# The threshold search of a two-step graph kernel: its second choice, its interpolation and its narrowing made by GpSimd on single columns

## What is computed

```
h = relu(layernorm(x))                       # x: 3327 x 256
S = adj + I;  Rf = S / rowsum;  Rb = S / colsum
for s in 0, 1:
    L = (Xa @ W1) @ W2 @ (Xa @ W3).T         # 3327 x 3327 logits
    A = softmax of L over the largest entries of each row
        that together hold 0.9 of the row's softmax
    Xf, Xb, Xa = Rf @ Xf, Rb @ Xb, A @ Xa
    Z += Xf @ U1[s] + Xb @ U2[s] + Xa @ U3[s]
x = x + layernorm(h + Z) * gamma + beta
x = x + attention layer of relu(layernorm(x))    # 8 heads, masked by adj
```

## Time and profile before

| | |
|---|---|
| median of 3 runs | 2310.26 us (2309.46 to 2310.35) |
| the profiled execution's own time | 2308.43 us |
| its span, first to last instruction | 2306.6 us |
| PE busy | 2132.9 us (92%) |
| DVE busy | 2046.8 us (89%) |
| ACT busy | 1943.6 us (84%) |
| POOL busy | 883.9 us (38%) |
| mean granted TensorE clock | 0.981 |

### The profile page before, as it was taken

How to read it: one execution, slowest core, us unless ns; L and a number is a source line. 1 busy time by engine, 2 the same in 40 slices (tenths; PEclk the granted TensorE clock), 3 DMA queues, 4 the chain that set the end, 5 groups by cost and what they waited for, 6 DMA issues and landing times.

```text
span 2306.6 us, 26328 instructions
## 1 busy us (share of the span) xinstructions
PE 2132.9 (92%) x8250; PEld 1376.1 (60%) x8250; DVE 2046.8 (89%) x3721; ACT 1943.6 (84%) x2849; POOL 883.9 (38%) x1247
## 2 busy tenths in 40 slices
PE   7599999999999998997999999999999999999975
PEld 4377777777777777443356555555555555555554
DVE  5699999999999998148859999999999999999995
ACT  4899999999999995257389899999999899899844
POOL 2134443344433442002224444444444444444432
PEclk9699999999999999999999999999999999999988
DMA  7255544555445552432321221221221221122242
GB/s 242 82 124 137 113 98 110 128 122 113 98 117 128 115 111 59 115 93 39 56 56 52 52 52 43 52 58 37 52 59 37 52 58 43 48 57 52 46 118 71
DMA packets 85168, 190.05 MB, mean 82 GB/s; under 512 B 12193, under 2 KB 65056, under 8 KB 85024
## 3 DMA queue, kind: packets, MB, share of 16 engines
q0 software_dynamic: 26208, 61.37, 16.8%
q1 hardware_dynamic: 56496, 125.48, 16.4%
q10 hardware_dynamic: 2320, 1.48, 0.2%
HBM read 154.19 MB, written 34.10 MB: 82 GB/s over the span
## 4 chain that ended last, share of the span: by engine, by line
DVE 45%; PE 4%; issue 1%; ACT 1%; POOL 0%; DVEq 0%; ACTq 0%; POOLq 0%
DVE junk L1941 19%; DVE small L1988 4%; DVE logits L1980 4%; DVE logits L2113 4%; DVE small L1884 4%; PE bank L1118 2%; DVE small L1969 1%; DVE small L1972 1%; DVE QT L2057 1%; PE bank L776 1%; DVE small L1993 1%; DVE small L1996 1%; PE bank L1180 1%; PE bank L1144 0%; PE bank L1100 0%
## 5 line engine op out<-in xcount | busy, mean ns | idle before, releaser
L1941 DVE SCALAR_TENSOR_TENSOR junk<-logits,small,expd 128x3327 uint8<-128x3327 f32 x184 | 677.9, 3684 | 4.7
L1144 PE MATMUL bank<-h_aug,turns 128*128 128x256 f32 x2704 | 629.8, 380 | 0.1
L1118 PE MATMUL bank<-both,pair 128*128 128x512 f32 x1352 | 610.9, 596 | 17.6 <-ACT sides L1494 17.6
L1144 PEld LDWEIGHTS bank<-h_aug,turns 128*128 128x128 f32 x2704 | 499.2, 190 | 95.2 <-issue 30.3
L1118 PEld LDWEIGHTS bank<-both,pair 128*128 128x128 f32 x1352 | 250.8, 190 | 302.2 <-issue 260.8
L1118 PE MATMUL bank<-h_aug,both 128*128 128x257 f32 x1352 | 316.7, 384 | 2.0 <-ACT sides L1477 1.6
L1118 PEld LDWEIGHTS bank<-h_aug,both 128*128 128x128 f32 x1352 | 251.0, 190 | 63.7 <-issue 26.9
L1100 PE MATMUL bank<-KTr,QT 64*128 64x512 f32 (+1 forms) x728 | 246.4, 613 | 44.3 <-ACT logits L1341 40.4
L1401 ACT ACTIVATE junk<-expd,small 128x3327 int8<-128x3327 f32 x88 | 270.1, 3069 | 1.5
L1407 ACT ACTIVATE junk<-expd,small 128x3327 int8<-128x3327 f32 x88 | 270.4, 3073 | 0.3
L1741 POOL TENSOR_TENSOR small<-small 128x1 f32<-128x1 f32 x52 | 14.4, 277 | 571.5 <-DVE small L2013 571.5
(11 more groups left out here) (259 smaller groups left out, 3120.2 us busy)
## 6 DMA issues: line engine op xcount, KB each, us to landing
both<-adj_turned SPq DMA_DIRECT2D x52, 832.0 KB, 6.8
both<-adj_turned POOLq DMA_DIRECT2D x52, 832.0 KB, 9.4
pair<-adj_turned SPq DMA_DIRECT2D x52, 832.0 KB, 4.5
z<-sides POOLq DMA_DIRECT2D x78, 128.0 KB, 3.1
spread<-sides POOLq DMA_DIRECT2D x26, 128.5 KB, 3.7
turns<-spread SPq DMA_DIRECT2D x26, 128.5 KB, 2.1
attended<-att_out SPq DMA_DIRECT2D x26, 128.0 KB, 8.7
expd<-attended SPq DMA_DIRECT2D x26, 128.0 KB, 2.1
```

The source lines that it names most:

```text
L1118: done = pe.matmul(SX[:, 0:width], half(t, h)[:, bass.ts(jj, P)], rows_of(j), start=(j == 0), stop=(j == T - 1))
L1144: last = pe.matmul(AB[:, 0:D], attT[i % 4][:, b, :], h_aug[:, g + b, 0:D], start=(g + b == 0), stop=(g + b == T - 1))
L1941: chain.did(dve.scalar_tensor_tensor(junk[:, 0:N], logits[t % 3][:, 0:N], col(t, "cand"), expd[t % NE][:, 0:N], ALU.is_gt, ALU.mult, accum ...
```

## The change

In step two, `start_search` leaves DVE. A new POOL function `model` waits for `searched_early`, moves the bracket's ends (`move_ends`, shared with `bracket`), interpolates and announces the first cut as `modelled`; DVE's `start_search` is only the wait for it. `narrow` is on POOL too and takes in the ten step widths; DVE's first `weigh` announces `weighed`, and DVE waits for `steps_ready` ahead of its second `weigh`. The reciprocal is a power of -1 there, the choice between ends is a product and a sum on single columns, and the bracket's width has the other sign. In step one the step widths (`make_steps`) are POOL's, made right behind `prepare`. In POOL's program of step two, `model(t+1)` stands ahead of `count_needed(t)`.

```diff
                     def bracket(t):
                         here, high, deep = pair(t, "point0"), pair(t, "high"), pair(t, "deep")
+                        pool.wait_ge(sem["probed"], t + 1)
+                        move_ends(t, here, high, deep)
+
+                    def move_ends(t, here, high, deep):
                         to_high, to_deep = pair(t, "top"), pair(t, "bottom")
-                        pool.wait_ge(sem["probed"], t + 1)
                         chain.did(pool.tensor_scalar(col(t, "part"), here[:, 1:2], 0.0, None, ALU.is_gt))
+                        chain.did(pool.tensor_tensor(to_high, here, high, ALU.subtract))
                         chain.did(pool.tensor_scalar(col(t, "part_up"), here[:, 1:2], 0.0, None, ALU.is_le))
-                        chain.did(pool.tensor_tensor(to_high, here, high, ALU.subtract))
                         chain.did(pool.tensor_tensor(to_deep, here, deep, ALU.subtract))
                         chain.wait()
-                        chain.did(pool.tensor_scalar(to_high, to_high, col(t, "part"), None, ALU.mult))
-                        chain.did(pool.tensor_scalar(to_deep, to_deep, col(t, "part_up"), None, ALU.mult))
-                        chain.wait()
-                        chain.did(pool.tensor_tensor(high, high, to_high, ALU.add))
-                        pool.tensor_tensor(deep, deep, to_deep, ALU.add).then_inc(sem["bracketed"], 1)
-                        chain.wait()
+                        for end, way, side in ((high, to_high, "part"), (deep, to_deep, "part_up")):
+                            for k in range(2):
+                                chain.did(pool.tensor_scalar(end[:, k:k + 1], way[:, k:k + 1], col(t, side),
+                                                             end[:, k:k + 1], ALU.mult, ALU.add))
+                        chain.wait()
+
+                    def model(t):
+                        high, deep, width = pair(t, "high"), pair(t, "deep"), pair(t, "width")
+                        point, part = pair(t, "point2", 0), col(t, "part")
+                        pool.wait_ge(sem["searched_early"], t + 1)
+                        move_ends(t, pair(t, "point1"), high, deep)
+                        chain.did(pool.tensor_tensor(width, high, deep, ALU.subtract))
+                        chain.did(pool.tensor_tensor(pair(t, "up", 0), deep[:, 0:1], high[:, 0:1], ALU.add))
+                        chain.wait()
+                        chain.did(pool.tensor_tensor(col(t, "rinv"), pair(t, "width", 1), constants[:, 14:15], ALU.pow))
+                        chain.wait()
+                        chain.did(pool.tensor_scalar(part, pair(t, "high", 1), col(t, "rinv"), -1.0, ALU.mult, ALU.mult))
+                        chain.wait()
+                        chain.did(pool.tensor_scalar(col(t, "part_up"), part, PUSH, -0.5, ALU.subtract, ALU.max))
+                        chain.wait()
+                        chain.did(pool.tensor_scalar(part, part, PUSH, col(t, "part_up"), ALU.add, ALU.min))
+                        chain.wait()
+                        chain.did(pool.tensor_scalar(point, pair(t, "width", 0), part, pair(t, "high", 0),
+                                                     ALU.mult, ALU.add))
+                        chain.wait()
+                        pool.tensor_scalar(col(t, "cand"), point, col(t, "max"), LN2 + 3e-5, ALU.add, ALU.add
+                                           ).then_inc(sem["modelled"], 1)
+                        chain.did(pool.tensor_tensor(pair(t, "d_bottom", 0), point, pair(t, "deep", 0), ALU.subtract))
+                        chain.did(pool.tensor_scalar(pair(t, "d_top", 0), point, -2.0, pair(t, "up", 0),
+                                                     ALU.mult, ALU.add))
+                        chain.did(pool.tensor_scalar(pair(t, "top", 0), pair(t, "width", 0), 0.5, None, ALU.mult))
+                        chain.wait()
+
+                    def narrow(t):
+                        bottom, excess = pair(t, "d_bottom", 0), pair(t, "d_top", 0)
+                        pool.wait_ge(sem["weighed"], t + 1)
+                        chain.did(pool.tensor_scalar(col(t, "move"), col(t, "mass"), col(t, "target"), None, ALU.is_ge))
+                        chain.did(pool.tensor_scalar(col(t, "cand"), bottom, -0.5, col(t, "cand"), ALU.mult, ALU.add))
+                        chain.wait()
+                        chain.did(pool.tensor_scalar(bottom, excess, col(t, "move"), bottom, ALU.mult, ALU.add))
+                        chain.did(pool.tensor_scalar(col(t, "cand"), pair(t, "top", 0), col(t, "move"), col(t, "cand"),
+                                                     ALU.mult, ALU.add))
+                        chain.wait()
+                        pool.tensor_scalar(steps_of(t), constants[:, 4:4 + 2 * late], bottom, None, ALU.mult
+                                           ).then_inc(sem["steps_ready"], 1)
 
                     def make_steps(t):
-                        pool.wait_ge(sem["narrowed"], t + 1)
-                        pool.tensor_scalar(steps_of(t), constants[:, 4:4 + 2 * late], pair(t, "d_bottom", 0), None,
-                                           ALU.mult).then_inc(sem["steps_ready"], 1)
+                        pool.wait_ge(sem["low_ready"], t + 1)
+                        pool.tensor_scalar(steps_of(t), constants[:, 4:4 + 2 * late], col(t, "low"), -0.5 ** early,
+                                           ALU.mult, ALU.mult).then_inc(sem["steps_ready"], 1)
...
                     if first_step:
                         prepare(0)
+                        pool.wait_ge(sem["setup"], 2 * late)
+                        make_steps(0)
                     else:
+                        chain.did(pool.memset(constants[:, 14:15], -1.0))
+                        chain.wait()
                         for t in range(T):
                             add_own(t)
                             if t == 2:
                                 prepare(0)
                             if t == 5:
                                 bracket(0)
+                            if t == 7:
+                                model(0)
                             if t == 8:
-                                make_steps(0)
+                                pool.wait_ge(sem["setup"], 2 * late)
+                                narrow(0)
                             if t == 9:
                                 prepare(1)
                             if t == 12:
                                 bracket(1)
                             if t == 15:
+                                model(1)
                                 count_needed(0)
                             if t == 16:
                                 settle(0)
-                                make_steps(1)
+                                narrow(1)
...
                         if t + 1 < T and (first_step or t > 0):
                             prepare(t + 1)
-                            if not first_step:
+                            if first_step:
+                                make_steps(t + 1)
+                            else:
                                 bracket(t + 1)
+                                model(t + 1)
                         if first_step or t > 0:
                             count_needed(t)
                             settle(t)
                             if not first_step and t + 1 < T:
-                                make_steps(t + 1)
+                                narrow(t + 1)
...
-                    def spans(t, width, halved):
-                        chain.did(dve.tensor_scalar(steps_of(t), constants[:, 4:4 + 2 * late], width, halved,
-                                                    ALU.mult, ALU.mult))
-
                     def start_search(t):
+                        if not first_step:
+                            dve.wait_ge(sem["modelled"], t + 1)
+                            return
                         dve.wait_ge(sem["searched_early"], t + 1)
                         dve.wait_ge(sem["prepared"], t + 1)
-                        if first_step:
...
+                        chain.did(dve.tensor_scalar(col(t, "cand"), pair(t, f"point{early}", 0), col(t, "max"),
+                                                    LN2 + 3e-5, ALU.add, ALU.add))
                         chain.wait()
 
                     def weigh(t):
-                        chain.did(dve.scalar_tensor_tensor(junk[:, 0:N], logits[t % 3][:, 0:N], col(t, "cand"),
-                                                           expd[t % NE][:, 0:N], ALU.is_gt, ALU.mult,
-                                                           accum_out=col(t, "mass")))
-                        chain.wait()
-
-                    def narrow(t):
...
                     def bisect(t, k):
-                        weigh(t)
                         if k == 0 and not first_step:
-                            narrow(t)
+                            weigh(t).then_inc(sem["weighed"], 1)
```

(6 more changed lines are left out.)

60 lines of the change are left out of this document (5 added, 55 removed).

## The result

The changed kernel takes 2381.81 us, the median of four runs (2380.01 to 2383.12), beside 2310.31 us for the kernel before in the same comparison: 1.0307 times as long, with an interval of 1.0294 to 1.032. That is 71.5 us slower. The forecast was 2362 us in a range of 2328 to 2392, with 0.88 on slower. The profiled execution took 2380.01 us, its span is 2378.2.

The account below looks back on a forecast made before the run. DVE was taken to set the pace, with PE the bound after 1.2 us per tile. Terms 43.7 + 3.9 + 1.3 + 6.6 - 3.4 made +52 us on 2308.4: 2360, as a median 2362; range 2328 to 2392.

Parts of the forecast that it names:

- The likeliest case: Step two, the forecast itself: a loss of 1.4 to 2.4 us per tile, 2350 to 2375 us; chance 52%.
- a dear power or a held cut: Rival: power over 0.7 us, or DVE waits for POOL's trailing instructions; +2.4 to +3.5 per tile, 2375 to 2402 us; 20%.
- The cut: Step two, `model` on POOL takes 4.7 us behind ACT's probe; first `weigh` starts earlier, gaining 0.53 us per tile.
- The held cut: Part of a 20% rival: DVE's `weigh` waits for POOL's trailing instructions, beginning up to 0.3 us later, 7 us in all.
- The keep: Step two, `weigh` to `keep`: one POOL instruction caught, `count_needed` queued behind; 6.95 us against 4.54, loss 2.4 per tile.
- The step widths: Step two, `narrow` on POOL finishes under the row maximum: no wait at second `weigh`, except last tile, about 1.3 us.
- The middle phase: Tiles 0 and 1 between the steps: `model` and narrowing on POOL delay DVE, +6.6 us (3 to 10).
- tile 2: Step two's differently starting tile: nothing of `model` hidden, `keep` later, less a 0.92 us wait for logits; +3.9 us.
- Step one: Step widths leave DVE, saving 0.13 us in each of 26 tiles: -3.4 us, or 0 if nothing is gained.
- POOL is not held: Rival: `count_needed` goes on under the `weigh`, `keep` comes 1.3 us earlier per tile; faster, 2282 us; 7%.

Follow-up runs that it names:

- run two: The changed kernel with POOL's power of -1 replaced by a product of the same operands, leaving out the reciprocal: 2371.98 us, 1.027 of the kernel before.

## Why the forecast came out as it did

The mechanism, the sign and the place of both waits were as forecast. The time was 19.8 us above the value given and inside the range (71.5 where the terms made 52.1). The likeliest case's own stretch (+1.4 to +2.4 per tile) was left upwards: 2.67 lies in the span of the rival "a dear power or a held cut", but neither of its two conditions was met: the power took 0.58 us where over 0.7 was asked for, and DVE's pass was not held.

- **The cut** was mis-sized. Forecast 4.7 us from the end of ACT's probe to the `weigh`, a gain of 0.53 per tile. Measured: ACT's row for L1422, which stands where L1430 stood, ends at 1607.05 + 0.39 = 1607.44, the `weigh` begins at 1612.85, 5.41 us. The power takes 0.58 us, 0.68 with its hand-over (L1736 to L1738), where an ordinary step of 0.34 was taken: 0.34 of the 0.7 too little. The four products of `move_ends` took 1.42 us (L1724 to L1733) where 1.24 was taken: 0.18 more. The other dependent steps came to 0.29 to 0.44 each, around the high step of 0.38: the rest. The forecast's upper bound of 5.4 us was meant for a power of 1 us; the chain came up to it with a power of 0.58. The gain became a loss: of the 2.67 per tile, 2.50 lie between the `weigh` and `keep`'s pass (7.69 for 5.19), and 0.17 here and in the rest of the tile. That is 0.70 x 23 = 16 of the 19.4 us by which the sum fell short; by run two the power alone is some 9 of them.
- **The held cut**, the rival's other condition, did not come. DVE's `weigh` begins 0.03 us behind the end of L1747 with L1749 in flight (0.04 in the run with the row maximum in its place), and takes 3.69 us as every other pass. L1759 runs 0.21 us into `keep`'s pass in 24 tiles, and that pass takes 3.68 to 3.69 us as before. The sentence of the Trainium skill that whoever starts first keeps the ports, by which the pass would begin up to 0.3 us later, stands in SBUF — State Buffer, Who interferes with whom, and not on the GPSIMD page at which the prediction points; it is not borne out here.
- **The keep** was right: 6.95 us forecast, 6.98 measured, with one instruction caught in 24 of the 26 tiles. `keep`'s small instructions take 0.71 us for 0.65. They wait for the same two signals as before, but the second one, `totalled`, is now late: POOL's L1798, which gives it, ends at 1620.24, and DVE's L2106 begins at 1620.27. Before, it lay ready 0.24 us ahead. That is 0.06 per tile, in no term of the forecast.
- **The step widths** were right: no wait but in the last tile (1.01 us; 1.3 forecast) and two in the middle phase.
- **The middle phase, tile 2 and step one together**: +9.07 up to tile 3's row maximum where the terms -3.4, +6.6 and +3.9 gave +7.1. The waits for `modelled` in the middle phase, with `gather` (L839) behind them, are the two named, 8.2 and 6.4 us (14.6 in the list above). The two profiles divide it. Step one: `keep`'s first reciprocal after it begins at 883.38 for 884.92, -1.5 for -3.4. The middle phase up to the end of tile 2's probe, 1198.90 for 1194.30: +6.1 for +6.6. Tile 2 from there to the row maximum, 16.62 for 12.15: +4.5 for +3.9. So step one is most of the 2 us too little. No run took the middle phase's loss away by itself.
- **Step one**: -3.4 forecast; by 884 us the kernel after is 1.5 us ahead. The wait for the widths was placed between the `weigh` and the instruction behind it, and from the start of the accumulator's read to that instruction it is 0.19 us, where step two's later `weigh`s, with no wait there, have 0.12 (the rows below). So it gives half of what it takes away. The run with the wait ahead of the `weigh` has the whole.

DVE after, first in step one with the wait ahead of L1965, then in step two without it:

```profile
523.47 3.69 DVE L1949 SCALAR_TENSOR_TENSOR junk<-logits,small,both 128x3327 uint8<-128x3327 f32 x1
527.08 0.09 DVE L1949 DVE_READ_ACCUMULATOR junk<-logits,small,both 128x1 f32 x1
527.27 0.27 DVE L1965 TENSOR_SCALAR small<-small 128x1 f32<-128x1 f32 x1
...
1586.18 0.08 DVE L1949 DVE_READ_ACCUMULATOR junk<-logits,small,expd 128x1 f32 x1
1586.30 0.27 DVE L1965 TENSOR_SCALAR small<-small 128x1 f32<-128x1 f32 x1
```

**The rivals.** "POOL is not held" would have given 2282 us; the run that takes the holding away without changing POOL's program gave 2294.65, so its condition was false, and its sum was 13 us too low besides, which the mis-sized cut, 0.70 per tile or 16 us, more than covers. Its threshold, 6.1 us a tile for what DVE waits and does in the two places, stands against 5.41 + 3.29 = 8.7 measured.

What stays open: why a pass that has begun holds a POOL instruction and a POOL instruction in flight doesn't visibly hold the pass. Those in flight reached at most 0.21 us into a two-input pass of DVE, whose length varies by about 0.02, and no run had a long POOL instruction in that place. It is open, too, whether the model in smaller pieces around the count would have paid.

## What to carry to other kernels

Before work is moved from a full engine to an idle one, read at what moment it must be done and what stands behind it in the idle engine's queue. Here the moved steps end just where the full engine starts a two-input pass, so one trailing instruction of 0.27 us was held for 3.7 us, and everything queued behind it was on the path. It was the queue and not the trailing trio that cost most: the trio put elsewhere gave back 0.9 us per tile, since the count was held in its place; the count taken out of the queue gave back 2.0. Trailing work that nobody waits for yet belongs behind the signal that somebody does wait for; but when it is put there, follow the queue once round to the next tile, since the lateness came back over a transfer, `prepare` and ACT's probe. Small pieces with cover (the narrowing, step one's widths) are worth moving, and their wait belongs where the engine still has work of its own ahead.

## What the runs showed of the hardware

- A GpSimd power on a single column takes 0.58 us (572 to 578 ns, 26 times), where a product in its place takes 0.19, and costs 0.40 us per tile more.
- A GpSimd instruction on single columns that is started within a two-input pass of VectorE ends 0.1 to 0.2 us behind the pass: L1750 takes 3.72 us for 0.27 under a one-input pass of nearly the same length, L1761 3.59 for 0.34 in the middle phase. The Trainium skill (SBUF — State Buffer, Who interferes with whom) says that a one-input reduction doesn't contend; the run with the row maximum in the pass's place agrees with its 0.27 us.
- One more wait for another engine's signal costs VectorE 0.07 us between two dependent instructions even if the signal came long ago, and nothing measurable ahead of a long pass (in step one 0.25 us from the accumulator's read, over one small instruction, to the `weigh`, with the wait there in the run with step one's widths alone and without it in the kernel after).
